# Row-interleaved transfers of a fused attention and feed-forward kernel, cut into four of 32 rows each, with the first tiles of the feed-forward fetched one a turn and the last stores put on two queues

## The chip, the cores and the metric

The kernel runs on one core of a Trainium2 chip. The metric is the device time of one execution in microseconds (us). The engines are TensorE (PE, with its weight loads as PEld), VectorE (DVE), ScalarE (ACT), GpSimd (POOL) and SyncE (SP). SP and ACT each have a DMA queue of their own, written SPq and ACTq in the profile; in the list of queues SP's is q1 and ACT's q10. Both feed the core's 16 DMA engines.

## The reference

The input x is 32 tiles of 128 rows by 512 columns in fp32. One layer is computed on it:

```python
x = x + tanh(g_xattn) * xattn(layernorm(x), ctx)   # 16 heads of 32, keys and values from the image part of ctx
x = x + tanh(g_ffn) * ffn(layernorm(x))
# ffn: h = relu(t @ up_w) ** 2                      512 -> 2048
#      y = h @ down_w + (t @ expert_w) * (sum of the two largest of t @ gate_w)
#      ffn = (y - mean) * rsqrt(var + eps) * gamma + beta
```

## The kernel before, in words

There are two stages, and each engine has its instructions written out in a fixed order in both.

**Attention** works on one tile of 128 rows in each turn (a "slot" in the code, NB = 32 tiles in all), in a software pipeline: in turn s TensorE multiplies weights for tile s + 1, forms the scores of tile s and applies the probabilities of tile s - 1. Products are made from high and low parts in three matmuls (`mm3`, lines 76 to 78). Most tiles are turned by way of DRAM: the normalised tile `xn`, the keys `kf` and the queries `qf` are stored in pieces of 32 elements to `xd_scratch`, `kd_scratch` and `qd_scratch`, fetched back as `x_dealt`, `k_dealt` and `q_dealt`, and turned within 32x32 blocks by VectorE (line 574). SP issues all of these transfers, in one fixed order for each turn: the residual `xres` (line 299), the finished tile to `x_scratch` (line 302), then `xd_scratch`, the input of a later tile (`xin`, line 270), `kd_scratch`, `x_dealt`, `qd_scratch`, `k_dealt`, the context `cin` and `q_dealt`. Up to turn 22, two stores of split weights to `ring_scratch` and one fetch of weights stand at the end of the turn. In turns 23 to 28 that place belongs to `load_first(sp, s - 23)`, which fetches what the feed-forward begins with.

**Feed-forward** works on eight groups of GB = 4 tiles. Its tile holds rows 4b, 4b + 1, ... "dealt" over the partitions: partition 32c + b holds row 4b + c. `dealt_rows(a)` is the access pattern `"(b c) n -> c b n"` with c = KT = 4, so the DRAM side of one such transfer has three dimensions, 4 x 32 x 512, with rows of 2 KB. It is used by `load_x` for the four tiles of group 0 (`fx<-x_scratch`, line 1184), by `load_res` for the residual tiles (line 1597) and by `store_out` for the results (`out_x<-fy`, line 1601). The four tiles of group 0 are normalised during attention: in turns 24 to 27 VectorE takes their means and variances (`stats`, line 1389), and GpSimd scales them. The pieces of the first feed-forward weights go into `fy` (`load_piece`, line 1191); pieces 0 and 1 are first read by GpSimd's `up_sums(0)` (line 1363 on `c`) in turn 28, and pieces 2 and 3 by `up_sums(1)` after the last full turn.

**The end.** In the last group ScalarE copies the four products to `y` (`fy`); then for each tile j VectorE adds the expert part (line 1837), takes the variance (1842, 1844), centres (1848), and with GpSimd's inverse root writes the result (`result`, line 1855), which raises the semaphore `dv_o`. SP waits for it and issues the store of that tile, then waits for all four stores (`after`). A transfer adds DMA = 16 to its semaphore.

Of the kernel before, what the change touches and what calls it, by code (L numbers as in the profile page):

```python
# [11 lines left out]
P = 128  # L12
D = 512
KT = D // P
# [6 lines left out]
DMA = 16  # L21
# [1029 lines left out]
def feed_forward_start(nc, whole, t, x2_dram, bank, ident, tanh_g, powers, W, fx, fy, pair, eight, ring_dram, at_least, mm3):  # L1051
# [5 lines left out]
    GB = D // P  # L1057
# [23 lines left out]
    c = [sb("c0", [P, 2, D])]  # L1081
# [12 lines left out]
    xn = [fx[:, n, :] for n in range(GB)]  # L1094
    y = [fy[:, n, :] for n in range(GB)]

    X_ORDER = (0, 2, 1, 3)
# [80 lines left out]
    def dealt_rows(a):  # L1178

        return a.rearrange("(b c) n -> c b n", c=KT)  # L1180

    def load_x(sp, g, j):
        if static(g) and g == 0:
            sp.dma_start(xn[j], dealt_rows(x2_dram[j])).then_inc(ld_x[j], DMA)
        else:
            sp.dma_start(xn[j], x2_dram[g * GB + j]).then_inc(ld_x[j], DMA)

# [9 lines left out]
    def load_first(sp, n):  # L1197
        if n == 0:
            q_stored(sp)
        if n < 2:  # L1200
            for pos in range(2 * n, 2 * n + 2):
                load_x(sp, 0, X_ORDER[pos])
        elif n < 4:
            for p in range(2 * n - 4, 2 * n - 2):
                load_piece(sp, p)
        elif n == 4:
            sp.dma_start(ga_raw[:, :, :], t["gate"].rearrange("p (k n) -> p k n", k=KT)).then_inc(ld_g, DMA)
            sp.dma_start(two_ident[:, :], t["two_ident"]).then_inc(ld_g, DMA)
        else:
            for src, dst in (("gamma", gamma), ("beta", beta)):  # L1210
                sp.dma_start(dst[:, :], t[src].broadcast_to([P, D])).then_inc(ld_g, DMA)
# [173 lines left out]

    def stats(dve, g, pos):
        j = X_ORDER[pos]
        at_least(dve, ld_x[j], g * DMA + DMA)
        dve.bn_stats(st6[:, :], xn[j]).then_inc(dv_bs, 1)
        at_least(dve, po_rs, g * GB + pos)  # L1390
        at_least(dve, dv_xn, g * GB + pos)
        at_least(dve, dv_bs, g * GB + (pos + 1), apart=True)
        dve.bn_aggr(mv[:, :], st6[:, :]).then_inc(dv_st, 1)
# [105 lines left out]
    start.pair_of, start.dealt_rows = pair_of, dealt_rows  # L1499
    start.hi_T, start.lo_T, start.turn, start.turn_blocks, start.upward = hi_T, lo_T, turn, turn_blocks, upward  # L1500
    start.stats, start.normalise, start.inv_std, start.prepare = stats, normalise, inv_std, prepare
    start.ring_first = ring_first
    start.split_gate_hi, start.split_gate_lo, start.load_first, start.load_piece, start.load_x = (
        split_gate_hi, split_gate_lo, load_first, load_piece, load_x)
    return start
# [2 lines left out]
def feed_forward(nc, ctx, block, ff, t, out, x2_dram, xn_dram, ring_dram, bank, ident, tanh_g, powers, dv_x2, st_x2,  # L1508
                 at_least, mm3):
    NB, NI, NE, GB, NQ, NC, NS, NT, H, static = ff.NB, ff.NI, ff.NE, ff.GB, ff.NQ, ff.NC, ff.NS, ff.NT, ff.H, ff.static  # L1510
    NGRP = NB // GB
# [51 lines left out]
    def ring_load(eng, g, n):  # L1563
        at_least(eng, ff.pe_R, g * NS + (n - KT + 1), apart=eng is nc.sync)
        i = n if is_last(g) else ff.ring_order[n]
        for m in range(2):
            eng.dma_start(ff.ring[n % KT][m].bitcast(F32), ring_dram[i, m]).then_inc(ff.ring_moved[n % KT], DMA)

    @block.sync
    def _(sp):  # L1570
        def before():
            for n in range(GB):
                next_x(0, n)

        def next_x(g, j):
            if is_first(g):
                sp.wait_ge(ff.pe_T, NT)
                sp.wait_ge(ff.po_t, 2 * GB)
            else:
                at_least(sp, ff.dv_tr, (g - 1) * NT + GB + (j + 1), apart=True)  # L1580
            ff.load_x(sp, g + 1, j)

        def out_blocks(g, i):
            if i < GB:
                at_least(sp, ff.po_t, g * (2 * GB) + (i // 2 + 1) * GB, apart=True)
                src = ff.y[i]
            else:
                src = ff.xn[i - GB]
            dst = xn_dram[i].rearrange("(i b) (c k d) -> (b c) k i d", i=HG, c=KT, k=KT)
            sp.dma_start(dst, src.rearrange("p (k i d) -> p k i d", k=KT, i=HG)).then_inc(ff.st_n[ff.pair_of(i)], DMA)  # L1590

        def in_blocks(g, i):
            at_least(sp, ff.st_n[ff.pair_of(i)], g * (2 * DMA), apart=True)
            sp.dma_start(ff.y[i] if i < GB else ff.xn[i - GB], xn_dram[i]).then_inc(ff.ld_t[ff.pair_of(i)], DMA)

        def load_res(g, j):
            sp.dma_start(res(g, j), ff.dealt_rows(x2_dram[g * GB + j])).then_inc(ff.ld_last if is_last(g) else ff.ld_r[j], DMA)

        def store_out(g, j):
            at_least(sp, ff.dv_o, g * GB + (j + 1), apart=True)  # L1600
            sp.dma_start(ff.dealt_rows(out[g * GB + j]), ff.y[j]).then_inc(ff.st_o[j], DMA)

        def group(g):
            first, last = is_first(g), is_last(g)
            for q in range(NQ):
                if first and q < NQ - 4:
                    for p in range(2 * q + 8, 2 * q + 10):
                        ff.load_piece(sp, p)
                if not first and q == 0:
                    if not last:  # L1610
                        for j in range(GB):
                            next_x(g, j)
                    for j in range(2):
                        load_res(g - 1, j)
                    if last:
                        for j in range(GB):
                            at_least(sp, ff.dv_tr, (g - 1) * NT + GB + (j + 1))
                            load_res(g, j)
                if not first and q in (2, 3):
                    store_out(g - 1, q - 2)  # L1620
                    load_res(g - 1, q)
                if not first and q == 4:
                    store_out(g - 1, 2)
                jj = q - (6 if first else 5)
                moved = [2 * jj, 2 * jj + 1, GB + jj, GB + jj + 2] if not last and jj in (0, 1) else []
                for i in moved:
                    out_blocks(g + 1, i)
                for i in moved:
                    in_blocks(g + 1, i)
                if not first and q == 4:  # L1630
                    store_out(g - 1, 3)
                if last and 0 < q < KT + 1:
                    k = q - 1
                    sp.wait_ge(ff.pe_P, (g * NQ + k + 1) * NC)
                    for m, w in enumerate((ff.u_hi, ff.u_lo)):
                        sp.dma_start(w[k][:, 0:D].bitcast(F32), ring_dram[NI + k, m]).then_inc(ff.ld_e, DMA)
            if not last:
                for n in range(NI + 2, NS):
                    ring_load(sp, g, n)
            if not last:  # L1640
                for n in range(KT):
                    ring_load(sp, g + 1, n)

        def after():
            for j in range(GB):
                store_out(NGRP - 1, j)
            for j in range(GB):
                sp.wait_ge(ff.st_o[j], NGRP * DMA)

        run(sp, group, before, after)  # L1650

# [84 lines left out]
    def _(act):  # L1736
# [27 lines left out]
        def group(g):  # L1764
            first, last = is_first(g), is_last(g)
            for q in range(NQ):
                if q > 1:
                    hidden_hi(g, 2 * q - 2)
                    hidden_hi(g, 2 * q - 1)
                if q == 1:  # L1770
                    logits(g)
                if first and q == 1:
                    freed(act)
                if not (first and q == 0):
                    ff.copy_1(act, g, q)
                    ff.copy_5(act, g, q)
                if q == 1:
                    hidden_hi(g, 0)
                    hidden_hi(g, 1)
                if q > 1:  # L1780
                    ring_load(act, g, 2 * q)
                    ring_load(act, g, 2 * q + 1)
                if first and q + 2 < NQ:
                    if q == 1:
                        freed(act)
                        stored(act)
                    ff.up_hi(act, q + 2, 0)
                    ff.up_hi(act, q + 2, 1)
                if first and q + 2 < NQ:
                    ff.up_hi(act, q + 2, 2)  # L1790
            hidden_hi(g, NI - 2)
            hidden_hi(g, NI - 1)
            if last:
                for j in range(GB):
                    evict(g, j)
                return
            ring_load(act, g, NI)
            ring_load(act, g, NI + 1)
            for i in range(GB):
                ff.hi_T(act, g + 1, i)  # L1800
            ff.hi_T(act, g + 1, GB)
            ff.hi_T(act, g + 1, GB + 1)
            weigh(g, 0)
            ff.hi_T(act, g + 1, GB + 2)
            weigh(g, 1)
            ff.hi_T(act, g + 1, GB + 3)
            weigh(g, 2)
            weigh(g, 3)
# [262 lines left out]
```

## Time and profile before

| | |
|---|---|
| median of three runs | 1335.82 us (1334.78 to 1336.01) |
| profiled execution | 1336.42 us |
| its span, first to last instruction | 1334.3 us |
| outside the span | 2.1 us |
| mean granted TensorE clock | 0.994 of full speed |
| TensorE matmul busy | 97% of the span |
| DVE, ACT, POOL busy | 72%, 44%, 39% |
| HBM read, written | 178.60 MB, 64.23 MB |

The span is what the trace covers, and all places in it are given in us from its start. The prediction works on the profiled execution and carries the difference over to the median, which lies 0.6 us below it.

### The profile page before, as it was taken

To read this page: it belongs to the slowest core of one execution; us is meant where nothing else is said; L and a number is where in the kernel's file an instruction comes from. 1 tells how busy PE (TensorE), PEld (TensorE's weight loads), DVE (VectorE), ACT (ScalarE), POOL (GpSimd) and SP (SyncE) were. 2 spreads that over 40 slices of the span, in tenths; PEclk is the share of its full clock that TensorE was granted. 3 is DMA by queue.
4 is the path that set the end of the run, shared out by engine and by line. 5 is a ranking of instruction groups with operands and counts; after the bars stand their busy time and mean duration, and the time that the engine had idled before them with its cause. 6 is when DMAs were issued, how large, how long until landed. Compare 5 with 4: busy or idle time off the path is not lost.

```text
span 1334.3 us, 27852 instructions
## 1 busy us (share of the span) xinstructions
PE 1295.1 (97%) x8924; PEld 1108.8 (83%) x8924; DVE 955.5 (72%) x1824; ACT 585.4 (44%) x1835; POOL 517.2 (39%) x671
## 2 busy tenths in 40 slices
PE   6999999999999998999999999999999999999996
PEld 4788888888887886888888888888998888888884
DVE  5677777777777767786776776766866866866664
ACT  4778777787777785322222212213213113113110
POOL 2566666666657874350240240230230230220111
PEclk9999999999999999999999999999999999999998
DMA  6389888999888744459368377377377377376541
GB/s 239 90 203 235 229 228 220 223 227 235 221 193 209 188 112 156 129 141 271 110 182 247 111 185 242 110 186 240 110 191 238 118 180 237 124 187 206 189 131 32
DMA packets 402747, 243.71 MB, mean 183 GB/s; under 512 B 303097, under 2 KB 303225, under 8 KB 402681
## 3 DMA queue, kind: packets, MB, share of 16 engines
q1 hardware_dynamic: 370424, 184.15, 52.1%
q10 hardware_dynamic: 32256, 58.73, 13.2%
q8 instruction: 35, 0.57, 0.2%
q14 instruction: 32, 0.25, 0.1%
HBM read 178.60 MB, written 64.23 MB: 182 GB/s over the span
## 4 chain that ended last, share of the span: by engine, by line
PE 75%; issue 8%; DVE 4%; DMA 4%; POOL 2%; SPq 2%; ACT 0%; ACTq 0%; DVEq 0%; POOLq 0%
PE bank L76 16%; PE bank L78 15%; PE bank L77 15%; PE wide L77 6%; PE wide L76 6%; PE wide L78 6%; PE bank L406 4%; PE wide L394 2%; PE bank L415 2%; DMA pair<-x_scratch 1%; DMA xn_scratch<-fx 1%; SPq L1590 1%; DMA k_dealt<-kd_scratch 1%; POOL yrstd L1963 1%; SPq L270 1%
## 5 line engine op out<-in xcount | busy, mean ns | idle before, releaser
L1738 ACT ACTIVATE hT_hi<-c 128x512 fp32r<-128x512 f32 x128 | 79.9, 631 | 408.7 <-PE wide L78 215.8
L1970 POOL TENSOR_TENSOR pair<-pair,beta 128x512 f32<-128x512 f32 x28 | 38.2, 1363 | 452.6 <-DMA pair<-x_scratch 452.6
L77 PE MATMUL wide<-wo_lo,hT_hi 128*128 128x512 f32 x512 | 203.4, 397 | 0.0
L78 PE MATMUL wide<-wo_hi,hT_lo 128*128 128x512 f32 x512 | 202.3, 395 | 0.0
L76 PE MATMUL wide<-wo_hi,hT_hi 128*128 128x512 f32 x512 | 202.0, 395 | 0.2 <-DMA wo_lo<-ring_scratch 0.2
L784 ACT ACTIVATE prob<-wide,nmx 128x128 f32<-128x128 f32 x512 | 182.0, 411 | 2.5 <-DVE nmx L595 2.5
L961 POOL TENSOR_TENSOR prob<-prob,rr 128x512 f32<-128x512 f32 x128 | 133.4, 1048 | 78.6 <-DVE rr L603 78.6
L1816 DVE TENSOR_TENSOR hT_lo<-c,hT_hi 128x512 fp32r<-128x512 f32 x128 | 100.0, 801 | 77.7 <-ACT hT_hi L1738 77.2
L784 ACT ACTIVATION_READ_ACCUMULATOR prob<-wide,nmx 128x1 f32 x512 | 129.0, 252 | 0.0
L78 PEld LDWEIGHTS wide<-wo_hi,hT_lo 128*128 128x128 f32 x512 | 96.3, 188 | 22.8
L76 PEld LDWEIGHTS wide<-wo_hi,hT_hi 128*128 128x128 f32 x512 | 96.5, 188 | 22.1 <-DMA wo_lo<-ring_scratch 0.7
L77 PEld LDWEIGHTS wide<-wo_lo,hT_hi 128*128 128x128 f32 x512 | 96.4, 188 | 20.8
L76 PE MATMUL bank<-wq_hi,up_hi 128*128 128x256 f32 x384 | 108.6, 283 | 3.0 <-DVE c L1446 3.0
L77 PE MATMUL bank<-wq_lo,up_hi 128*128 128x256 f32 x384 | 107.8, 281 | 0.0
L78 PE MATMUL bank<-wq_hi,up_lo 128*128 128x256 f32 x384 | 107.8, 281 | 0.0
L595 DVE TENSOR_REDUCE nmx<-wide 128x4 f32<-128x512 f32 x128 | 82.1, 683 | 13.3 <-PE wide L394 13.3
L1473 DVE SCALAR_TENSOR_TENSOR c<-c 128x512 f32<-128x512 f32 x128 | 85.1, 706 | 0.0
L76 PE MATMUL bank<-wv_hi,up_hi 128*128 128x256 f32 x288 | 81.0, 281 | 0.4 <-DVE c L1467 0.2
L78 PE MATMUL bank<-wv_hi,up_lo 128*128 128x256 f32 x288 | 81.2, 282 | 0.0
L77 PE MATMUL bank<-wv_lo,up_hi 128*128 128x256 f32 x288 | 80.9, 281 | 0.0
L758 ACT ACTIVATE pT<-bank 128x512 f32<-128x512 f32 x122 | 66.0, 598 | 33.3 <-PE bank L406 33.3
L76 PEld LDWEIGHTS bank<-wq_hi,up_hi 128*128 128x128 f32 x384 | 72.4, 189 | 4.2 <-DVE c L1446 4.2
(234 smaller groups left out, 3476.7 us busy)
## 6 DMA issues: line engine op xcount, KB each, us to landing
wo_hi<-ring_scratch ACTq DMA_DIRECT2D x110, 256.0 KB, 3.6
wo_lo<-ring_scratch ACTq DMA_DIRECT2D x110, 256.0 KB, 4.6
wo_hi<-ring_scratch SPq DMA_DIRECT2D x46, 256.0 KB, 2.7
wo_lo<-ring_scratch SPq DMA_DIRECT2D x46, 256.0 KB, 3.0
fx<-x_scratch SPq DMA_DIRECT2D x36, 256.0 KB
xin<-in_x SPq DMA_DIRECT2D x32, 256.0 KB, 3.3
cin<-in_ctxT SPq DMA_DIRECT2D x32, 256.0 KB, 3.0
xres<-in_x SPq DMA_DIRECT2D x32, 256.0 KB, 3.7
```

Source lines behind the costliest of these rows:

```text
L76: eng.matmul(dst, ah, bh, start=first and k == 0, stop=False)
L77: eng.matmul(dst, ah, bl, start=False, stop=False)
L78: mm = eng.matmul(dst, al, bh, start=False, stop=last and k == n - 1)
L406: mm = pe.transpose(cols(btp(a, g), h), prob[par][:, g, h * P:(h + 1) * P], ident[:, :])
L595: dve.tensor_reduce(nmx[:, g * HG:(g + 1) * HG], bank[g].rearrange("p (h k) -> p h k", h=HG), AX.X, ALU.max, negate=True).then_inc(dv_mx, 1)
L758: return act.activation(dst, src, ACT.Copy)
L784: i = act.activation(prob[par][:, g, h * P:(h + 1) * P], cols(bank[g], h), ACT.Exp, bias=nmx[:, n:n + 1], scale=1.0, accum_out=rs[:, n:n + 1])
L961: pool.tensor_tensor(p, p, r, ALU.mult).then_inc(po_p, 1)
L1473: dve.scalar_tensor_tensor(out=cc[:, m, :], in0=cc[:, m, :], scalar=0.0, in1=cc[:, m, :], op0=ALU.max, op1=ALU.mult).then_inc(dv_h, 1)
L1738: return act.activation(dst, src, ACT.Copy)
L1816: dve.tensor_tensor(ff.hT_lo[i % 2][:, :], ff.c[i // 2 % 2][:, i % 2, :], ff.hT_hi[i % 2][:, :].bitcast(F32), ALU.subtract).then_inc(ff.dv ...
L1970: pool.tensor_tensor(res(g, j), res(g, j), ff.beta[:, :], ALU.add).then_inc(ff.po_r, 1)
```

## The change

There is a new helper `quarters(tile, rows)`: it gives the four pairs of 32 partitions of a tile and the 32 DRAM rows that belong on them. It is used in two of the three places that had `dealt_rows`:

- `load_x` for group 0 issues four transfers of 32 rows instead of one of 128. The semaphore `ld_x[j]` therefore reaches 4 x 16, and `stats` waits for that.
- the stores of the last group are four transfers a tile: SP issues the first two (`store_last(sp, j, 0)`), and ACT, after its last copies, the other two (`store_last(act, j, 1)`). The final wait counts them all.
- `load_first` is laid out anew over the turns:

| turn | before | after |
|---|---|---|
| 23 | x tiles 0, 2 | x tile 0 |
| 24 | x tiles 1, 3 | x tile 2 |
| 25 | pieces 0, 1 | x tile 1, piece 0 |
| 26 | pieces 2, 3 | x tile 3, piece 1 |
| 27 | gate weights, two_ident | pieces 2, 3, gate weights, two_ident |
| 28 | gamma, beta | gamma, beta |

The residual loads and the stores of the seven other groups keep `dealt_rows`.

```diff
+    def quarters(tile, rows):
+
+        return [(tile[m * P // KT:(m + 1) * P // KT, :], rows.rearrange("(b c) n -> c b n", c=KT)[m]) for m in range(KT)]
+
     def load_x(sp, g, j):
         if static(g) and g == 0:
-            sp.dma_start(xn[j], dealt_rows(x2_dram[j])).then_inc(ld_x[j], DMA)
+            for dst, src in quarters(xn[j], x2_dram[j]):
+                sp.dma_start(dst, src).then_inc(ld_x[j], DMA)
         else:
             sp.dma_start(xn[j], x2_dram[g * GB + j]).then_inc(ld_x[j], DMA)
...
         if n == 0:
             q_stored(sp)
-        if n < 2:
-            for pos in range(2 * n, 2 * n + 2):
-                load_x(sp, 0, X_ORDER[pos])
-        elif n < 4:
-            for p in range(2 * n - 4, 2 * n - 2):
+        if n < GB:
+            load_x(sp, 0, X_ORDER[n])
+            if n > 1:
+                load_piece(sp, n - 2)
+        elif n == GB:
+            for p in range(2, GB):
                 load_piece(sp, p)
-        elif n == 4:
             sp.dma_start(ga_raw[:, :, :], t["gate"].rearrange("p (k n) -> p k n", k=KT)).then_inc(ld_g, DMA)
...
-        at_least(dve, ld_x[j], g * DMA + DMA)
+        at_least(dve, ld_x[j], g * DMA + KT * DMA)
...
+    def store_last(eng, j, part):
+
+        eng.wait_ge(ff.dv_o, (NGRP - 1) * GB + (j + 1))
+        for src, dst in ff.quarters(ff.y[j], out[(NGRP - 1) * GB + j])[2 * part:2 * part + 2]:
+            eng.dma_start(dst, src).then_inc(ff.st_o[j], DMA)
...
         def after():
             for j in range(GB):
-                store_out(NGRP - 1, j)
+                store_last(sp, j, 0)
             for j in range(GB):
-                sp.wait_ge(ff.st_o[j], NGRP * DMA)
+                sp.wait_ge(ff.st_o[j], (NGRP - 1 + KT) * DMA)
...
             if last:
                 for j in range(GB):
                     evict(g, j)
+                for j in range(GB):
+                    store_last(act, j, 1)
                 return
```

## Rows read from the trace of the kernel before

**Rows 1.** The page's busy times by engine: busy us, share of the span, instructions

```profile
PE 1295.1 (97%) x8924; PEld 1108.8 (83%) x8924; DVE 955.5 (72%) x1824; ACT 585.4 (44%) x1835; POOL 517.2 (39%) x671
```

**Rows 2.** Chain that ended last, from 381 us: start us, us, what

```profile
381.16 1.75 PE bank L406 x16
...
395.43 4.00 SPq L270
399.47 3.95 DMA kd_scratch<-kf
403.44 4.04 DMA k_dealt<-kd_scratch
...
428.73 1.75 PE bank L406 x16
...
443.78 1.75 PE bank L406 x16
```

**Rows 3.** Waits between 380 and 500 us: who for whom, total us, times, longest

```profile
DVE kT L574 <- DMA k_dealt<-kd_scratch: 5.2, 2, 2.8
```

**Rows 4.** Windows by turn: length, busy by engine, PEclk, DMA share, GB/s

```profile
336.00:351.00 15.00, 15.00 (x130) 12.48 (x128) 11.31 (x21) 11.75 (x45) 10.16 (x14) 1.00 0.93 229
...
411.20:426.30 15.10, 13.92 (x124) 11.28 (x123) 10.77 (x23) 10.59 (x42) 10.68 (x14) 1.00 0.78 191
426.30:441.30 15.00, 15.00 (x129) 12.48 (x128) 12.38 (x25) 11.23 (x44) 13.19 (x16) 1.00 0.95 249
```

**Rows 5.** Timeline of SP's queue, turns 20, 23 and 27: start us, us

```profile
345.11 0.48 SPq L1149 DMA_DIRECT2D fx<-in_ex  x1
...
389.42 1.35 SPq L1184 DMA_DIRECT2D fx<-x_scratch  x2
...
392.44 0.60 SPq L302 DMA_DIRECT2D x_scratch<-x  x1
394.75 0.64 SPq L196 DMA_DIRECT2D xd_scratch<-xn  x1
...
451.39 1.16 SPq L1207 DMA_DIRECT2D ga_raw<-in_gate  x1
```

**Rows 6.** DMA engines, 389 to 399 us: busy tenths in 40 slices

```profile
DMA  9973669755241256885999982222899995222222
```

**Rows 7.** Timelines of DVE and POOL: first use of x tile 0 and of piece 0

```profile
398.48 0.67 DVE L1389 BATCH_NORM_STATS2 fst<-fx 128x6 f32<-128x512 f32 x1
...
463.61 0.74 POOL L1363 TENSOR_TENSOR c<-fy 128x256 f32<-128x256 f32 x1
```

**Rows 8.** Issues by tile: duration in ns, min/median/max, first and last start

```profile
L1149 SPq DMA_DIRECT2D fx<-in_down x16: 354/355/433, 51.4 to 285.2; - x16
L1184 SPq DMA_DIRECT2D fx<-x_scratch x4: 596/606/692, 389.4 to 406.8; - x4
```

**Rows 9.** Timelines of DVE and SP's queue in the last 16 us

```profile
1325.50 0.75 DVE L1855 SCALAR_TENSOR_TENSOR fy<-fy,yrstd,fx 128x512 f32<-128x512 f32 x1 [0.52 <-issue]
...
1318.89 7.92 SPq L1601 DMA_DIRECT2D out_x<-fy  x4
```

**Rows 10.** Windows after the last result; columns as in group 4

```profile
1330.00:1331.00 1.00, 0.00 (x0) 0.00 (x0) 0.00 (x0) 0.00 (x0) 0.00 (x0) 0.50 0.26 102
...
1333.20:1333.40 0.20, 0.00 (x0) 0.00 (x0) 0.00 (x0) 0.00 (x0) 0.00 (x0) 0.50 0.08 31
1333.40:1333.80 0.40, 0.00 (x0) 0.00 (x0) 0.00 (x0) 0.00 (x0) 0.00 (x0) 0.50 0.00 0
```

**Rows 11.** DMA, 509 to 516 us: busy tenths in 40 slices; issues, median us to landing

```profile
DMA  0000000000000089889720300000000000000000
...
x_scratch<-x SPq DMA_DIRECT2D x1, 256.0 KB, 2.8
```

**Rows 12.** All stores to x_scratch by line 302: time to landing

```profile
DMA to landing us min/median/max: 2.0/3.2/7.1
```

**Rows 13.** ACT's ring loads by line 1567, durations in ns as in group 8

```profile
L1567 ACTq DMA_DIRECT2D wo_lo<-ring_scratch x110: 450/453/1789, 546.7 to 1297.5; - x110
```

More of the change, by code:

```diff
@@ L1501, in feed_forward_start @@
     start.stats, start.normalise, start.inv_std, start.prepare = stats, normalise, inv_std, prepare
-    start.ring_first = ring_first
+    start.ring_first, start.quarters = ring_first, quarters
     start.split_gate_hi, start.split_gate_lo, start.load_first, start.load_piece, start.load_x = (
```

## Prediction

> **What bounds the kernel now.** I read five views in this order. The page's busy times come first [rows 1]: TensorE's matmuls cover 97% of the span and no other engine passes 72%, so only a stretch in which TensorE stands still can give time back. The change touches DMA transfers in two places, so I looked for such stretches there.
>
> The chain of work that ended last gives TensorE's pace [rows 2]. The 16 transposes of line 406 come once a turn. From 428.73 to 443.78 a turn takes 15.05 us; from 381.16 to 428.73 three turns take 47.57, where 3 x 15.05 = 45.15. So 2.42 us are lost in the two turns behind the four dealt loads. In between the chain leaves TensorE: it goes through SP's issue of `xin`, which holds SP's queue for 4.00 us, then the store of the keys (3.95) and their fetch (4.04). The list of waits has its end: VectorE stood idle for `k_dealt` twice, 5.2 us in all [rows 3]; part of that is slack, and 2.42 us reach TensorE. The windows show the loss as PE busy for 13.92 of 15.10 us, at a DMA share of 0.78, below the 0.93 and 0.95 of turns without loss [rows 4]. So the 16 engines as a whole weren't short; something held a few of them.
>
> The strip of DMA shares shows what [rows 6]. After the pair of dealt loads at 389.42 [rows 5] there is a stretch at 1 to 2 tenths and later two at 2 tenths: about 4 of 16 engines still work through their part, and a transfer issued behind, which needs all 16, waits for these four.
>
> The second place is the end. The last result is written at 1325.50 + 0.75 = 1326.25; four issues go from 1318.89 to 1326.81, each right behind its result, and the last takes about 0.53 us [rows 9]. Then nothing computes, and the DMA share stands at 0.26 with 102 GB/s up to 1333.4 [rows 10]. 0.26 x 16 is 4 engines. One tile of 262144 bytes takes 2.57 us at that rate, four take 10.3, and they pile up. From the last result to the last packet there are 7.1 us, and then 1334.3 - 1333.4 = 0.9 to the end of the span.
>
> **What 16 engines would do.** The trace has a transfer of a tile to DRAM with nothing beside it, `x_scratch<-x` at 510 us: shares of 8 and 9 tenths for nine slices of 0.175 us, landed 2.8 us after its issue [rows 11]. Over all stores of that line the time to landing goes from 2.0 to 7.1, median 3.2 [rows 12]. No 32-row transfer of the new shape is in the trace. That it uses all 16 engines is a reading of the shapes: the dealt pattern has 4 as its outermost size and shows 4 engines; cut by c, a transfer has 32 rows outermost. The Trainium skill ("DMA: Bandwidth & Descriptors", section on why a DMA increments its semaphore by 16) says that the number of engines is the largest up to 16 that divides the slowest dimension of both sides: 4 before, 16 after. By that rule the trace agrees for the 4, and no row shows the 32.
>
> **Part 1: loads in quarters, spread over turns.** Removed: four issues of 0.606 us [rows 8]. Added: sixteen. The cost c of one is not in the trace; nearest rows are the strided two-dimensional load at 0.354, the dealt one at 0.606 [rows 8] and ACT's 0.450 [rows 13]. I take 0.45, with 0.35 and 0.61 as ends. A tile then costs SP 1.4 to 2.4 us, 1.8 as I take it, against 1.35 for the pair now [rows 5]. That lies in front of `xres` and of the store of `x`, which waits for VectorE until 392.44. In turns 25 and 26 a piece (0.48, the load of weights at 345.11 [rows 5]) comes on top. SP's next step that matters for the path is the store of `xn` at 394.75, 5.33 us after 389.42. With 0.60 each for `xres` and the store of `x`, and 0.48 for the piece, 3.65 us are left for four quarters, so it stays on time up to c = 0.91. The cost on the path is nothing; with the cover gone it would be what c exceeds 0.91 by, four times, in four turns. Turn 27 gets two pieces in front of the gate weights: 2 x 0.48 + 1.16 [rows 5] + 0.5 for the small one is 2.6, below 5.33 - 1.20 = 4.1.
>
> Removed with it: 2.42 us of stall. How much comes back? At most 2.42, at least nothing, if the queue is held up as much. I take all of it: up to turn 22 the same place of SP's order held three whole-tile transfers, the last issued at 345.11 [rows 5], and the window of turn 20 and its neighbours shows PE busy for 15.00 of 15.00 us [rows 4]. The new turns add one tile (24), or a tile and a piece (25 to 27), less than that. The window at 426.30 is the second witness: with the pairs of pieces it runs at 0.95 and PE loses nothing.
>
> Are the later fetches in time? x tile 0 is first read at 398.48 [rows 7], 9.1 us after its issue at 389.42. Each tile n is now issued at the end of turn 23 + n and read in turn 24 + n, so all four have that margin, less 3c = 1.4 for the last quarter: 7.7 us against landings of 2.0 to 7.1 in full traffic [rows 12]. A miss would stop VectorE, then TensorE once past the slack. Piece 0 is read at 463.61 [rows 7], a good 40 us after turn 25; pieces 2 and 3 later still. Nothing there.
>
> **Part 2: the last stores.** Removed: the pile on 4 engines. Added: two issues on SP and two on ACT for each tile, ACT being idle by then. For the last tile both queues issue at 1326.28 and again c later; the last quarter lands L after its own issue. L is 2.0 at least, 2.8 for the whole tile alone, 3.2 at the median under traffic [rows 11, 12]. A quarter is shorter, but four run together; I take 2.5. The last packet comes at 1326.28 + 0.45 + 2.5 = 1329.2 instead of 1333.4: 4.2 us gained. Ends: 1326.28 + 0.35 + 2.0 = 1328.6, gain 4.8, and 1326.28 + 0.61 + 3.2 = 1330.1, gain 3.3. The tile before is issued 1.3 us earlier and should be all but out of the way. The 0.9 us behind it stay.
>
> **Sum.** 2.42 + 4.2 = 6.6 us off the profiled 1336.42 gives 1329.8; off the median 1335.82 it gives 1329.2, 0.49% less. A difference of 0.2%, 2.7 us, is about what a measurement of this kernel can tell from no change.
>
> **Rivals.**
>
> *Only the end gains.* The turns stay late because the queue itself, not its four engines, is what the loads hold up, with SP issuing 16 pieces instead of 4. For: `xin`'s issue blocks SP's queue, and blocking may depend on the number of transfers before it. Against: turns with three transfers there run at pace [rows 4, 5]. Time: 1335.82 - 4.2 = 1331.6, still faster by 0.3%.
>
> *Only the front gains*, or the end little: quarters of 32 partitions run no quicker than the dealt tile did, so the last tile still takes 2.57 us behind its forerunners, at 102 GB/s. That is also the case in which the change does not spread the transfers, with the front helped only by having one tile a turn instead of two. Against: the lone store at 8 to 9 tenths [rows 11]. Time: 1335.82 - 2.4 = 1333.4 with the whole front, 1334.6 with half of it; on the border of no difference.
>
> *Slower: transfers of one queue do not overlap.* Each quarter then costs its own 2.0 us or more in line. At the end each queue has eight from 1318.89: 1318.89 + 8 x 2.0 = 1334.9 for the last packet, 1.5 later than now; at 2.8 it is 1341.3, 7.9 later. In front, four in line are 8 us or more per turn in the queue's way, more than the pair's present stall. It decides from 14.5 / 8 = 1.8 us a transfer. Time: 1335.8 + 1.5, plus at least the kept 2.42, which is no loss against before: 1337.3 to 1343.7. Against: 229 GB/s over a turn of 15 us is 3.4 MB or 13 tiles, which at 2.0 each would take 26 us [rows 4, 12]; so transfers do overlap. The Trainium skill ("DMA: Bandwidth & Descriptors", section on bandwidth) speaks for this side: it advises batches of 1 MiB or more and calls transfers below 64 KB descriptor-dominated, and these are 64 KB. Its fixed 2.0 us and 436 GB/s would give an estimated 2.15 us a quarter; paid once behind the last issue that ends near 1328.9, paid in line it is this rival. No row here shows which for quarters.
>
> **How the numbers follow.** Forecast (both places gain, 1328.2 to 1331.0): 0.76. Only the end: 0.11. Only the front, or the end little: 0.08. Slower, by the queue or a late tile: 0.03; 0.02 for no net change. The range takes the forecast's bounds (gains 0 to 0.2 beyond 2.42 and 3.3 to 4.8, and 0.6 for a measurement's own spread on either side) and the first rival: 1327.9 to 1332.1. Faster by over 0.2% is the forecast, the first rival and part of the second: 0.90. Within: 0.07. Slower: 0.03.
>
> **What would show it.** In the profile after: turns of 15.05 us throughout from 381 to 444; no wait of VectorE for `k_dealt`; `xin` issues of 1 to 2 us instead of 4.00; quarter issues near 0.45; DMA at 8 or 9 tenths for short moments behind each last result; last packet about 3 us behind the last result, not 7.1. Wrong if a new wait `fst<-fx` on DMA appears, if DMA stands at 2 tenths at the end again, or if the turns stay at 16.

## The result, and the profile after

The changed kernel takes 1329.35 us (median of six runs, 1327.11 to 1329.93), beside 1335.91 us for the kernel before (1334.04 to 1336.44) on the same chips. The ratio is 0.9937, interval 0.9922 to 0.9953. The medians differ by 6.6 us, which is the sum in the prediction, and 1329.35 lies inside its range of 1327.9 to 1332.1. By the ratio it is 8.4 us (0.0063 x 1335.82), and 1327.4, a little beyond the low end of that range. The ratio's interval goes from 1325.4 to 1329.5 us, so it holds both the forecast of 1329.2 and times that the range left out. The profiled execution has a span of 1327.3 us, 7.0 less.

The chain that ended last between 366 and 460 us answers to [rows 2]:

```profile
381.31 1.75 PE bank L406 x16
...
396.37 1.75 PE bank L406 x16
...
426.47 1.75 PE bank L406 x16
...
441.53 1.75 PE bank L406 x16
```

Three turns take 426.47 - 381.31 = 45.16 us, where it was 47.57. TensorE no longer leaves the chain, and all 2.41 us are back. VectorE's wait for `k_dealt` (5.2 us in [rows 3]) is one of 0.4, and there is none on `fst<-fx`:

```profile
DVE kT L574 <- DMA k_dealt<-kd_scratch: 0.4, 1, 0.4
```

The DMA share is not what changed. The second of these turns has PE busy all the time at a share as low as that of the turns with the loss (0.78 in [rows 4]):

```profile
396.40:411.40 15.00, 15.00 (x130) 12.47 (x129) 11.61 (x23) 11.22 (x44) 12.07 (x16) 1.00 0.79 193
```

SP's queue in turns 23 and 25, to be read beside [rows 5]:

```profile
389.53 2.63 SPq L1189 DMA_DIRECT2D fx<-x_scratch  x4
...
392.85 0.60 SPq L302 DMA_DIRECT2D x_scratch<-x  x1
394.90 0.60 SPq L196 DMA_DIRECT2D xd_scratch<-xn  x1
395.55 1.00 SPq L270 DMA_DIRECT2D xin<-in_x  x1
...
419.19 2.55 SPq L1189 DMA_DIRECT2D fx<-x_scratch  x4
421.79 0.42 SPq L1196 DMA_DIRECT2D fy<-in_up  x1
```

Four quarters cost SP 2.5 to 2.8 us rather than the 1.8 I took, because in each turn one of the four took longer (1.0 to 1.4 us). The cover held: the store of `xn` goes out at 394.90, beside 394.75 before, and `xin` takes 1.00 us, not 4.00. The issues grouped by tile and by line (duration in ns, min/median/max) give the price of one quarter:

```profile
L1189 SPq DMA_DIRECT2D fx<-x_scratch x16: 346/424/1418, 389.5 to 436.4; - x16
```

```profile
L1578 SPq DMA_DIRECT2D out_x<-fy x8: 315/388/442, 1317.0 to 1324.7; - x8
L1578 ACTq DMA_DIRECT2D out_x<-fy x8: 373/416/445, 1317.0 to 1324.8; - x8
```

The DMA shares at the end (40 slices from 1316 to 1328 us, 0.3 us each) show every tile leaving in a burst of its own at 8 or 9 tenths, where [rows 10] had a flat 2 to 3 tenths; the last two bursts all but touch:

```profile
DMA  0000008995000000889500000059963997100000
```

The last result and what follows it, by timeline and by windows (columns as in [rows 10]):

```profile
1323.61 0.75 DVE L1868 SCALAR_TENSOR_TENSOR fy<-fy,yrstd,fx 128x512 f32<-128x512 f32 x1 [0.51 <-issue]
```

```profile
1325.50:1326.00 0.50, 0.00 (x0) 0.00 (x0) 0.00 (x0) 0.00 (x0) 0.00 (x0) 0.50 0.96 262
...
1326.20:1326.40 0.20, 0.00 (x0) 0.00 (x0) 0.00 (x0) 0.00 (x0) 0.00 (x0) 0.50 0.22 72
1326.40:1326.60 0.20, 0.00 (x0) 0.00 (x0) 0.00 (x0) 0.00 (x0) 0.00 (x0) 0.50 0.00 0
```

The result ends at 1324.36, the last packet at 1326.4, the span at 1327.3. That is 2.94 us behind the last result, where it was 8.05: 5.1 us gained. The last result itself comes 1.9 us earlier than before's 1326.25, not 2.4; the feed-forward took 0.5 us more in this execution. 1.9 + 5.1 is the 7.0 of the spans.

### The profile page after: what moved, and what is told of

Read it like the earlier page. It is cut to its first block, busy times and chain, and to the rows that moved or that the text cites. A ratio compares the mean times of both kernels' runs of the same rounds, so it can differ in the third digit from the quotient of the medians.

```text
span 1327.3 us, 27876 instructions
## 1 busy us (share of the span) xinstructions
PE 1295.6 (98%) x8924; PEld 1110.7 (84%) x8924; DVE 954.8 (72%) x1824; ACT 585.0 (44%) x1835; POOL 518.1 (39%) x671
## 4 chain that ended last, share of the span: by engine, by line
PE 82%; issue 8%; DVE 5%; POOL 2%; ACT 1%; DMA 1%; ACTq 0%; SPq 0%; DVEq 0%; POOLq 0%
PE bank L76 17%; PE bank L78 16%; PE bank L77 16%; PE wide L77 7%; PE wide L78 7%; PE wide L76 7%; PE bank L406 4%; PE wide L394 3%; PE bank L415 2%; DMA prob<-in_wk 1%; DVE c L1478 1%; POOL yrstd L1976 1%; DVE yst L1855 1%; PE wide L1675 0%; DMA wo_lo<-ring_scratch 0%
```

## The experiments

All edits are on the changed kernel unless it says otherwise. "The end" is the time from the last result to the end of the span; "three turns" are those from 381 us. The diffs show the part of the edit that matters; the semaphore counts that go with it are left out. The six kernels spread_whole, quarters_paired and the four named end_ but end_only were executed once each, so only stages of their traces are read and not their times.

### Each part alone

**front_only**: the last stores as before.

```diff
             for j in range(GB):
-                store_last(sp, j, 0)
+                store_out(NGRP - 1, j)
...
-                for j in range(GB):
-                    store_last(act, j, 1)
```

> Loads in quarters, one tile a turn; the last four stores as before. Theory (two separate gains): every turn from 381 to 444 us takes 15.05 us, as in the changed kernel; from the last result to the end of the span it is 8.0 us as before; time about 1.9 to 2.4 us below before, ratio 0.998 to 0.9985, which the measurement can hardly tell from none. Rival (the front's gain is given back later): the turns are at pace but the last result comes within 0.5 us of before's 1326.25.

Measured: ratio 1.0004 (0.9987 to 1.0021), 12 runs from 1330.77 to 1343.28. In the trace three turns take 45.16 us and the end 8.15. The place behaves as expected; the time doesn't show it, and the forecast of 0.998 to 0.9985 lies outside the interval. The profiled execution's last result came at 1320.45, 5.8 us before that of the kernel before, so the rival isn't seen there either. Of the 5.8 us the three turns give 2.4, and 3.4 come in the feed-forward, which this edit doesn't touch: it differs by more from one execution to the next than the front is worth.

> The same kernel as front_only once more, since 12 runs of it showed no gain though its turns were at pace. Theory (the stall is gone for good and chance in the feed-forward covered it): 2 us below before, ratio 0.9985. Rival (what the front gains is lost again later, every time): ratio 1.000 or above.

Measured, with the same kernel: 0.9982 (0.9968 to 0.9996), 12 runs. This time the gain shows, 2.4 us, at the size of the stall. The two measurements of one kernel differ by 0.0022, more than the front is worth.

**end_only**: the loads of group 0 and their turns as before.

```diff
-            for dst, src in quarters(xn[j], x2_dram[j]):
-                sp.dma_start(dst, src).then_inc(ld_x[j], DMA)
+            sp.dma_start(xn[j], dealt_rows(x2_dram[j])).then_inc(ld_x[j], DMA)
...
-        if n < GB:
-            load_x(sp, 0, X_ORDER[n])
+        if n < 2:
+            for pos in range(2 * n, 2 * n + 2):
+                load_x(sp, 0, X_ORDER[pos])
```

> Stores of the last group in quarters on two queues; loads and their turns as before. Theory: three turns take 47.57 us as before; from the last result to the end of the span 2.9 us instead of 8.0; time 5.1 us below before, ratio 0.9962. Rival (the end's gain depends on the front): less than 4 us.

Measured: 0.9967 (0.9952 to 0.9981), 4.4 us; the end takes 3.02 us. Three turns take 47.3 us:

```profile
381.17 1.75 PE bank L406 x16
...
428.48 1.75 PE bank L406 x16
443.58 1.75 PE bank L406 x16
```

So the end's gain doesn't need the front.

### Which half of the front's edit does it

**spread_whole** keeps the new turns and fetches each tile whole; **quarters_paired** keeps the quarters and goes back to the old turns, by the two halves of the diff above.

> The changed kernel with its four loads whole again (dealt, four engines), one tile a turn. Theory (four engines busy for 2.6 us a tile, so the hold-up grows with what is queued on them): the lag of a single tile is half that of a pair and mostly within the slack; the five turns from 381 lose 0 to 0.8 us in all. Rival 1 (a fixed loss per dealt tile, 2.42 / 4 = 0.6 us): 2.4 us lost, 0.6 in each of four turns. Rival 2 (only their number in one turn counts): nothing lost.

> The changed kernel with quarters but the turns of before: two tiles, eight transfers, in turns 23 and 24, pieces in 25 and 26. Theory (all 16 engines work): turns stay at 15.05, loss 0 to 0.3 us, although SP spends 8 x 0.42 = 3.4 us or more on issues. Rival (SP's queue of issues is what holds the turn up): 8 issues in a turn cost as much or more than the pair, 0.9 to 1.5 us in each of the two turns.

Measured in spread_whole, chain that ended last:

```profile
381.17 1.75 PE bank L406 x16
...
426.32 1.75 PE bank L406 x16
441.38 1.75 PE bank L406 x16
```

Nothing is lost (45.15), and VectorE never waits for `k_dealt`, though by its shape each tile still runs on four engines. The issue of `xin` behind the first of them takes 0.98 us, where it took 4.00 behind the pair:

```profile
395.44 0.98 SPq L270 DMA_DIRECT2D xin<-in_x  x1
```

The theory (0 to 0.8 us lost) and the second rival (only the number in one turn counts) both allow for this, and this run alone can't tell them apart; the first rival is out. In quarters_paired three turns take 45.16 too. SP spends 4.62 us on the eight issues and VectorE waits 3.0 us in three places, which the slack takes up:

```profile
DVE kT L574 <- DMA k_dealt<-kd_scratch: 3.0, 3, 1.4
```

```profile
389.45 4.62 SPq L1189 DMA_DIRECT2D fx<-x_scratch  x8
```

Either half alone removes the whole stall. Two tiles in one turn cost nothing when their transfers use more engines, so their number alone isn't what counts either. What is left is the theory: in these turns four engines could be one tile (2.6 us) behind without loss, but not two.

### What sets the end

**end_halves** stores each last tile in two transfers of 64 rows, outermost size 2, one on each queue; **end_whole_two_queues** stores the tiles whole, 0 and 2 from SP, 1 and 3 from ACT; **end_one_queue** has SP issue all four quarters; **end_eighths** cuts to 16 rows, four on each queue.

```diff
-        for src, dst in ff.quarters(ff.y[j], out[(NGRP - 1) * GB + j])[2 * part:2 * part + 2]:
-            eng.dma_start(dst, src).then_inc(ff.st_o[j], DMA)
+        c0, c1 = 2 * part, 2 * part + 2
+        src, dst = ff.y[j][c0 * P // KT:c1 * P // KT, :], ff.dealt_rows(out[(NGRP - 1) * GB + j])[c0:c1]
+        eng.dma_start(dst, src).then_inc(ff.st_o[j], DMA)
```

> The changed kernel with each last tile stored in two transfers of 64 rows, outermost size 2, one on SP and one on ACT. Theory (the outermost size sets the number of engines): 2 engines for each; if both use the same two, the DMA share is 0.13 and the four tiles need 20 us, so 13 to 15 us from the last result to the end; if each takes its own two, 8 us. Rival (fewer rows a transfer or two queues help): 4 to 6 us.

> The changed kernel with the last four tiles stored whole (dealt), 0 and 2 by SP, 1 and 3 by ACT. Theory (both queues feed the same four engines for this shape): 8.0 us from the last result to the end, as before. Rival (each queue brings its own engines or share): 5 us or less.

Windows of end_halves, then of end_whole_two_queues:

```profile
1328.00:1330.00 2.00, 0.00 (x0) 0.00 (x0) 0.00 (x0) 0.00 (x0) 0.00 (x0) 0.50 0.13 51
...
1338.00:1340.00 2.00, 0.00 (x0) 0.00 (x0) 0.00 (x0) 0.00 (x0) 0.00 (x0) 0.50 0.13 51
```

```profile
1328.00:1329.00 1.00, 0.00 (x0) 0.00 (x0) 0.00 (x0) 0.00 (x0) 0.00 (x0) 0.50 0.26 102
```

A share of 0.13 is 2 of 16 engines, at 51 GB/s, half of the 102 in [rows 10]. So both queues' halves ran on the same two, and the end takes 17.4 us (1342.3 less the last result at 1324.93), 2.4 more than the longest that was expected. Whole tiles on two queues never pass a share of 0.27, with 47 to 102 GB/s in the windows of 1 us up to 1330: the end takes 8.85 us, 0.8 more than with one queue. Where the 2.4 and the 0.8 come from is open. A second queue brings no engines; the outermost size does. The Trainium skill ("DMA: Bandwidth & Descriptors", the section named in the prediction) says that a transfer from SP or ACT on fewer than 16 engines takes the lowest-numbered ones; the two queues sharing two engines agree with it.

> The changed kernel with all four quarters of each last tile issued by SP. Theory (quarters give the gain, the second queue only saves two issues of 0.42 us): from the last result to the end of the span 2.9 + 0.8 = 3.7 us. Rival (the second queue gives the gain): 6 to 8 us.

> The changed kernel with 16 rows a transfer, eight a tile, four on each queue. Theory: issues of 0.42 us set the end, so two more a queue and tile make it 2.9 + 0.8 = 3.7 us; a tile costs a queue 1.7 us against 3.06 us between results, so nothing piles up. Rival (a fixed cost of about 2 us a transfer in line): over 15 us.

end_one_queue takes 4.2 us at the end, a window of its last stores stands at 0.60 and 145 GB/s; end_eighths takes 4.4.

```profile
L1578 SPq DMA_DIRECT2D out_x<-fy x16: 314/424/429, 1321.1 to 1330.4; - x16
```

```profile
1329.00:1331.00 2.00, 0.00 (x0) 0.00 (x0) 0.00 (x0) 0.00 (x0) 0.00 (x0) 0.50 0.60 145
```

One queue issues 65536 bytes in 0.424 us, 155 GB/s: from here on the issues are the limit, not the engines. Both came out 0.5 to 0.7 us above the expected 3.7, and no run says why. Finer cuts aren't better: eighths take 1.5 us more at the end than quarters on the same two queues. Eight transfers a tile on two queues don't stack up at 2 us each, so the rival of transfers in line falls.

### The dealt transfers that the change left alone

In the traces so far the six groups between the second and the last gate product vary from 593.3 to 596.7 us, and VectorE waits for GpSimd's inverse root six times. GpSimd stands behind the residual tile, which SP fetches dealt right behind a dealt store. In the changed kernel, for the third tile of a group:

```profile
1142.22 0.63 SPq L1612 DMA_DIRECT2D out_x<-fy  x1
1143.07 0.56 SPq L1608 DMA_DIRECT2D pair<-x_scratch  x1
```

```profile
1154.26 1.29 POOL L1983 TENSOR_TENSOR pair<-pair,beta 128x512 f32<-128x512 f32 x1 [12.86 <-DMA pair<-x_scratch]
```

From the issue of that load to its first use 11.2 us pass. The DMA shares show why (40 slices from 1142 to 1156 us, 0.35 each): for 7 us they stand at 1 to 3 tenths.

```profile
DMA  0259999996952312222312222222222399799999
```

**res_quarters** fetches the residual tiles of all groups in quarters; **all_quarters** stores all groups so as well; **all_but_front** is all_quarters with the loads of group 0 whole and in pairs, as before the change.

```diff
-            sp.dma_start(res(g, j), ff.dealt_rows(x2_dram[g * GB + j])).then_inc(ff.ld_last if is_last(g) else ff.ld_r[j], DMA)
+            for dst, src in ff.quarters(res(g, j), x2_dram[g * GB + j]):
+                sp.dma_start(dst, src).then_inc(ff.ld_last if is_last(g) else ff.ld_r[j], DMA)
```

> The changed kernel with the residual tiles of every group fetched in quarters too. In the traces so far a group of four takes 98.57 us at best and up to 100.7, and where it is longer, VectorE waits at about 28 us of the group for GpSimd behind the residual tile. Theory (these dealt loads, queued behind dealt stores on four engines, make the groups long): fewer long groups, 1 to 3 us less than the changed kernel, ratio to before 0.992 to 0.995. Rival (the length comes from elsewhere): as the changed kernel, 0.9937 to 0.996.

> As res_quarters, with the stores of all groups in quarters too: nothing runs on four engines any more. Theory: groups at 98.6 to 98.8 us each, 3 to 5 us less than the changed kernel, ratio to before 0.990 to 0.993, and less spread between runs. Rival (SP's 4 x 0.42 us of issues for each tile delay the ring of weights or the turned tiles): groups of 99.5 us or more.

> As all_quarters, but with the four loads of group 0 whole and two a turn as before. If the groups' lengths no longer vary, the front's worth can be read from times: theory 2.4 us slower than all_quarters (ratio higher by 0.0018). Rival (given back): the same time as all_quarters.

Measured: res_quarters 0.9915 (0.9899 to 0.9930), all_quarters 0.9923 (0.9908 to 0.9939), all_but_front 0.9958 (0.9944 to 0.9972). The first two intervals overlap that of the changed kernel (0.9922 to 0.9953), so the times alone show no gain over it. The stages do. In all_quarters the load of the same residual tile, in four issues, is first used 5.3 us behind the first of them, not 11.2:

```profile
1141.97 1.85 SPq L1609 DMA_DIRECT2D pair<-x_scratch  x4
```

```profile
1147.23 1.29 POOL L1985 TENSOR_TENSOR pair<-pair,beta 128x512 f32<-128x512 f32 x1 [7.92 <-DMA pair<-x_scratch]
```

The list of waits from 632 to 1224 us has VectorE behind GpSimd's root for 18.5 us in the changed kernel, for 5.8 in res_quarters (second fence), and not at all in all_quarters:

```profile
DVE fy L1868 <- POOL yrstd L1976: 18.5, 6, 3.6
```

```profile
DVE fy L1869 <- POOL yrstd L1977: 5.8, 6, 1.6
```

The copies of the gate product (ACT) mark the groups, in the changed kernel and in all_quarters:

```profile
632.41 0.59 ACT L1749 ACTIVATE lg<-wide 16x512 f32<-16x512 f32 x1 [4.34 <-PE wide L1675]
...
1227.19 0.59 ACT L1749 ACTIVATE lg<-wide 16x512 f32<-16x512 f32 x1 [4.34 <-PE wide L1675]
```

```profile
632.21 0.59 ACT L1751 ACTIVATE lg<-wide 16x512 f32<-16x512 f32 x1 [4.34 <-PE wide L1677]
...
1223.61 0.59 ACT L1751 ACTIVATE lg<-wide 16x512 f32<-16x512 f32 x1 [4.34 <-PE wide L1677]
```

Six groups take 591.4 us, 98.57 each, where the changed kernel took 594.8: of the 18.5 us of waits, 3.4 had reached the groups' length. The theory holds in these groups. But from the last mark to the last result it is 99.0 us instead of 97.2, which is why all_quarters isn't faster than res_quarters.

all_but_front was meant to price the front, but its trace differs from all_quarters in two places. Of the 5.0 us between the spans (1330.5 and 1325.5), 2.4 are there by the first of these marks (634.60 and 632.21), the six groups are alike, and another 2.4 come behind the last mark: 101.5 us to the last result, where it was 99.0. In the first 10 us of that stretch TensorE is busy for 8.26 and its granted clock is 0.83:

```profile
1226.04:1236.04 10.00, 8.26 (x52) 8.03 (x53) 6.98 (x18) 2.39 (x5) 1.53 (x3) 0.83 0.46 143
```

So in the traces half of the difference between these two kernels is not the front's; whether it comes with the old front each time or was chance in this execution is not shown.

**late_residuals** is all_quarters with the last group's residual tiles fetched one a block of the up-projection; **late_but_front** has the old front on top.

```diff
-                    if last:
-                        for j in range(GB):
-                            at_least(sp, ff.dv_tr, (g - 1) * NT + GB + (j + 1))
-                            load_res(g, j)
...
+                if last and q > 3:
+                    at_least(sp, ff.dv_tr, (g - 1) * NT + GB + (q - 3))
+                    load_res(g, q - 4)
```

> As all_quarters, but in the last group the four residual tiles are fetched one a block of the up-projection, from the fifth on, and not all at its start. all_quarters took 99.0 us from the last group's gate product to the last result, against 97.0 in the others. Theory (its 16 + 16 quick transfers at the start of the group hold up the rings of weights or the copies there): 97.0 us again, ratio to before 0.989 to 0.991. Rival (the 2 us are from elsewhere in the group): 98.5 to 99.5 us, ratio 0.992.

> As late_residuals, with the four loads of group 0 whole and two a turn as before. Theory: the front is worth its 2.4 us of stall, ratio higher than late_residuals by 0.0018. Rival A (it is worth nothing in time): the same. Rival B (worth more than its stall, as all_but_front less all_quarters suggested): higher by 0.003 or more.

Measured: 0.9935 (0.9916 to 0.9955) and 0.9942 (0.9923 to 0.9961). The last stretch is 97.75 us in both, so crowding at the start of the last group explains 1.3 of the 1.8 us. The ratio missed its forecast of 0.989 to 0.991, and in time nothing is won over all_quarters. The profiled execution of late_residuals was already 2.4 us later than the changed kernel at its 366th microsecond, before any of these edits acts, which shows how much of a single time is not the kernel's doing.

**What the front is worth in time.** Five comparisons change the front alone: 1.0004 and 0.9982 against the kernel before; 0.9937 against end_only's 0.9967; 0.9923 against all_but_front's 0.9958; 0.9935 against late_but_front's 0.9942. They give -0.04, 0.18, 0.30, 0.35 and 0.07%, on average 0.17% or 2.3 us. Their intervals are 0.14% and more on each side. Only the second (0.04 to 0.32%) and the fourth can be told from no gain, and of the fourth half lies outside the front in the traces; the first, at -0.21 to 0.13%, leaves out the stall's own 0.18%. That the mean is near the stall of the traces (2.2 to 2.9 us in the four traces with the old front) is a consistency, not a measurement to the tenth; they don't share one set of runs of before either.

## Why the prediction came out as it did

*Bound and cause of the front's stall*: right. Four engines behind, `xin` held in SP's queue, `kd_scratch` and `k_dealt` late, VectorE, TensorE: 2.41 us were to be had, and all came. The second rival's half (one tile a turn suffices) is true for the front: spread_whole shows that cutting wasn't needed there. The prediction had named that only within a rival and didn't ask what spacing alone does. One of its signs was none: it saw the loss in a DMA share of 0.78 too, and the changed kernel has a turn at 0.79 without loss.

*SP's cost*: c was 0.42 against my 0.45, but one issue of each four takes longer, 2.5 to 2.8 us a tile against 1.8. It lay in the cover as forecast. The price that I gave for going beyond the cover was too high: even 4.62 us in quarters_paired cost TensorE nothing.

*The later fetches*: in time, no wait on `fst<-fx`.

*The last stores*: right in kind, and this is the step that failed, the term of the sum that was mis-sized: 4.2 us forecast, 5.1 measured (ends of 8.05, 8.15 and 8.11 us with dealt stores on one queue, of 2.9 to 3.1 in the nine traces with quarters on two queues). I took L = 2.5 from the rows on landing [rows 11, 12] and compared the sum with the last packet of before. Measured from the second issue of the last tile, about 1324.8, the last packet is at 1326.4, so L is 1.6. Part of the 0.9 us between them was counted twice: a landing comes later than the last packet, and the 0.9 us behind the last packet hold that already. For the whole tile in [rows 11], issued at 510.22 in the kernel before, the windows show the packets ending at about 512.6, 2.4 us behind the issue, where it landed after 2.8:

```profile
512.50:512.60 0.10, 0.10 (x2) 0.09 (x2) 0.10 (x2) 0.10 (x1) 0.10 (x1) 1.00 0.33 123
512.60:512.70 0.10, 0.10 (x3) 0.10 (x3) 0.10 (x1) 0.10 (x1) 0.10 (x1) 1.00 0.02 0
```

That is 0.4 of the 0.9. The rest is that quarters are through sooner than I took them to be. I had also read that strip of shares wrongly: 8 and 9 tenths stand in five slices, then 7 and 2, not in nine, so the lone tile's packets took 1.2 us and not 1.6. The estimate of 2.15 us a quarter was no term of the sum; the page of the Trainium skill gives its 2.0 us and 436 GB/s as a fit for transfers that GpSimd issues, and these are issued by SP and ACT.

*The sum*: 2.4 + 5.1 = 7.5 us is a ratio of 0.9944, inside the measured interval, and would have put the time at 1328.3, inside the range. The prediction's 6.6 was short by the 0.9 of that term; as 0.9951 it is inside the interval too. Between 7.5 and the 8.4 us of the ratio lie another 0.9 that no stage of the traces shows and that the runs' spread covers: that the ratio's time fell just beyond the range is in part chance, and so is the hit of the medians on 6.6. The width was mis-set too: I took 0.6 us for the runs' own spread from three of them, while 12 and 23 runs of one kernel went over 12 and 9 us. And its ends don't quite follow from the terms: gains of 2.62 and 4.8 and the 0.6 give 1327.8, the first rival and the 0.6 give 1332.2; the measured 1327.4 lies outside these as well.

*The rivals*: "only the end gains" is out by the turns, though a single timed comparison (front_only) looked like it. "Transfers of one queue don't overlap" is out by end_eighths. That a second queue adds nothing by itself is shown by end_whole_two_queues; what it adds once each transfer uses all engines is 4.2 - 2.9 = 1.3 us, of which two issues fewer in line (2 x 0.42) explain 0.8; the rest is open.

## What to carry to other kernels

Look at the outermost size of a transfer's access pattern before its bytes: 4 gave 4 engines of 16, 2 gave 2, and once two such tiles were queued together, what stood behind them waited for these few. Find such transfers by a DMA share that stays at 0.13 or 0.26 while a queue is backed up; either cut them along that dimension or space them out, whichever is cheaper on the issuing queue (0.42 us for each piece here), and look at all of them, not only where the chain shows a stall: the ones left alone cost 3.4 us over six groups in the traces. Doing it everywhere isn't free: the last group lost 1.8 us of that again. When a gain is smaller than the spread of the runs, read it from the stage in the trace and use the times only as a check.

## What the runs showed of the hardware

- Transfers issued from SP and from ACT with outermost size 2 shared the same two engines: 51 GB/s together, share 0.13 (end_halves).
- One queue could issue 64 KB quarters every 0.42 us, 155 GB/s (end_one_queue), and the 16 engines stood at a share of 0.60 then: there the issues and not the engines set the rate.
- From the issue of the last 64 KB quarter to its last packet 1.6 us passed, and 0.9 from there to the end of the span.
- In the eleven traces in which the residual tiles are fetched whole, the feed-forward's six groups take 593.3 to 596.7 us, and that variation vanished when no transfer in those groups was dealt: 591.4 us in all four traces of all_quarters, all_but_front, late_residuals and late_but_front. The last stretch kept its own, 97.75 to 101.5 us in these four.
